# Causal mask of an attention block as one bf16 product per PSUM bank, and its score products 64 rows deep on the two halves of the TensorE rows

## The chip, the cores and the metric

One NeuronCore of one Trainium2 chip runs the whole program. The metric is the device time of one execution in microseconds (us). Names used below: PE is the matmul side of TensorE and PEld its weight loads, DVE is VectorE, ACT is ScalarE, POOL is GpSimd, SP is the engine that queues most DMAs. Each engine works through its own instructions in order; semaphores tie the engines together.

## The reference

A small language model layer: a token lookup, a bidirectional state-space block (32 sequences of 512 tokens), and then a transformer layer. Its attention is the part that the change touches. For every position of the 512, attention runs over the 32 sequences, with 4 key/value groups of 4 query heads each, head size 16:

```
qkv = ln1 @ qkv_weight.T            # ln1: layer norm of h
scores = einsum('bgqsd,bgtd->bgqst', q, k) * 16**-0.5
scores = where(tril, scores, finfo.min)
attn = softmax(scores)
ao = einsum('bgqst,bgtd->bgqsd', attn, v)
h1 = h + ao @ proj_weight.T
# then layer norm, router, top 2 of 8 experts, and the experts
```

## The kernel before, in words

Three stages follow one another: the state-space stage, the attention stage (`attention_stage`), and the expert stage, with a small routing stage ahead of the experts. The attention stage takes the 512 positions in 32 turns of BB = 16 positions. In a turn the functions named `slot` on each engine set the order by hand; the engines overlap work of neighbouring turns.

TensorE in a turn `slot(c)`: `scores(c)` (L1395), `turn_v(c)` (transposes of the values, L1385), `qk(c+1)` (projections of the next turn, L1376), `turn2(c-1)` (transposes of the normalised rows of the turn before, L1445), `ranks(c-2)` (L1466, L1468), `router(c-1)` (L1454), `turn_p(c)` (transposes of the probabilities, L1405), `products(c)` (L1424), `project(c)` (L1433), `turn1(c+2)` (L1366).

One score product treats one position: the stationary operand is `qt`, (64 + 32) rows by 128 columns (4 query heads of a group times 32 sequences), the moving operand is `kb`, (64 + 32) rows by 128 (4 groups times 32 sequences). The first 64 rows are the 4 groups of 16 head values, with the groups that don't belong set to zero in `kb`; the last 32 rows hold an identity in `qt` and the causal mask in `kb`, so that the product adds the mask. POOL writes these 32 rows once, ahead of the turns. Four positions share one PSUM bank `A[i]`; the four banks are done in the order BANKS = (2, 3, 0, 1), and each raises `s_ps` at its end. In the profile a f32 product is two instructions, so a turn has 32 of them.

VectorE: `add_projection(c-1)` (L1570), `stats2(c-1)` (L1576, L1580), `less_max` of the first two banks (L1542, L1545), `v_copy` (L1533), `normalise2(c-1)` (L1590), `less_max` of the other two banks, `sums` (L1552, L1555), `keep_logits(c-1)` (L1597), `next_rows` and `place` for the routing, `stats1(c+2)` (L1510), `first_input`, `pick_experts`, `normalise(c+2)` (L1525).

ScalarE: `exp` of the first two banks (L1279), four `q_copy(c+1)` (L1259, PSUM to `qt`, 64x512 each), `exp` of the other two banks, `x2t_copy(c-1)` (L1303), four copies of `k_copy(c+1)` with a scale column (L1267, PSUM to `kb`), `pt_copy(c)` (L1286), `vs_copy(c+1)` (L1274), `ao_copy(c)` (L1297, eight of 64x256), `lt_copy(c+2)` (L1251).

GpSimd: `scales2(c-1)` (L1192, L1194), `base(c-1)` (L1209), `normalise(c)` (L1203), `scales1(c+2)` (L1183 to L1187), and `send(c-2)`, eight indirect DMAs (L1216).

The waits around the change: `scores(c)` waits for all nine copies of its turn on the semaphore `qk_ok` (QK = 9) and raises `s_ps` four times; `products(c)` also counts `qk_ok`, since it overwrites the banks that `q_copy` reads; `less_max` waits for `s_ps`.

Of the kernel before, what the change touches and what calls it, by code (L numbers as in the profile page):

```python
# [19 lines left out]
BF16 = mybir.dt.bfloat16  # L20
I32 = mybir.dt.int32
U32 = mybir.dt.uint32
ALU = mybir.AluOpType
ACT = mybir.ActivationFunctionType
AX_X = mybir.AxisListType.X

P = 128
# [932 lines left out]
BB = 16  # L960
NG = 4
NQ = 4
HD = 16
S_A = 32
NE = 8
QK = NQ + NG + 1
QT = 3
BANKS = (2, 3, 0, 1)
AV_BANK = (0, 1, 3, 2)
V_BANK = (2, 3)  # L970
GD = NG * HD
# [10 lines left out]
MASKED = -2.0 ** 127  # L982


def attention_stage(nc, w, h1_dram, out, xd_dram, both_all):
# [8 lines left out]
    with ctx:  # L994
        def sb(name, shape, dt=F32):
            return ctx.enter_context(nc.sbuf_tensor(name, shape, dt))
# [4 lines left out]
        lnw = sb("a_lnw", [P, 2, KD])  # L1001
        lnb = sb("a_lnb", [P, 2, KD])
        ident = sb("a_ident", [P, P])
        cmask = sb("a_cmask", [P, S_A])
        vmask = sb("a_vmask", [P, NG * HD])
        gmask = sb("a_gmask", [GD, NG])
        nh = sb("a_nh", [P, TT])
# [7 lines left out]
        r1 = sb("a_r1", [P, NCH * TT])  # L1015
        core = sb("a_core", [P, TT, DM])
        lt = sb("a_lt", [P, KD, SEQ])
        qt = sb("a_qt", [GD + S_A, BB, NQ, S_A])
        kb = sb("a_kb", [GD + S_A, BB, NG, S_A])
        vs = sb("a_vs", [P, BB, NG, S_A])  # L1020
        vb = sb("a_vb", [P, BB, NG * HD])
        ss = sb("a_ss", [P, BB, NG, S_A])
# [36 lines left out]
        A = [ctx.enter_context(nc.psum_tensor(f"a_pa{i}", [P, SEQ], F32)) for i in range(4)]  # L1059
        B = [ctx.enter_context(nc.psum_tensor(f"a_pb{i}", [P, SEQ], F32)) for i in range(4)]  # L1060
# [4 lines left out]
        S = {n: ctx.enter_context(nc.semaphore("a_" + n)) for n in names}  # L1065
# [11 lines left out]
        def after(eng, name, value):  # L1077

            if not (isinstance(value, int) and value <= 0):
                eng.wait_ge(S[name], value)  # L1080
# [44 lines left out]
        def _(pool):  # L1125
# [4 lines left out]
            for tile, value in ((ident, 0.0), (cmask, 0.0), (vmask, 0.0), (gmask, 1.0)):  # L1130
# [11 lines left out]
                               pattern=[[-1, P]], channel_multiplier=1).then_inc(S["c0"], 1)  # L1142
            pool.wait_ge(S["c0"], done + 1)
            done += 1
            rows = slice(GD, GD + S_A)
            pool.affine_select(out=cmask[rows, :], in_=cmask[rows, :], compare_op=ALU.is_ge, fill=MASKED, base=0,
                               pattern=[[-1, S_A]], channel_multiplier=1).then_inc(S["c0"], 1)
            pool.wait_ge(S["c0"], done + 1)

            for n, (tile, of) in enumerate(((kb, cmask[rows, :]), (qt, ident[rows, rows]))):  # L1150
                pool.tensor_copy(tile[rows].rearrange("p b g t -> p (b g) t"),
                                 of.unsqueeze(1).to_broadcast([S_A, BB * NG, S_A])).then_inc(S["c0"], 1)
                pool.wait_ge(S["c0"], done + 2 + n)
            done += 3
            for q in range(NQ):
# [89 lines left out]
        def _(act):  # L1245
# [8 lines left out]
            def q_copy(c, q):  # L1254

                act.wait_ge(S["qk_ps"], QT * c + q // 2 + 1)
                after(act, "s_ps", 4 * c)
                rows = slice(GD * (q % 2), GD * (q % 2 + 1))
                act.activation(qt[0:GD, :, q, :], B[q // 2][rows, :].rearrange("p (b s) -> p b s", b=BB), ACT.Copy  # L1259
                               ).then_inc(S["qk_ok"], 1)  # L1260

            def k_copy(c):

                act.wait_ge(S["qk_ps"], QT * (c + 1))
                after(act, "s_ps", 4 * c)
                for g in range(NG):
                    act.activation(kb[0:GD, :, g, :], B[2][0:GD, :].rearrange("p (b s) -> p b s", b=BB), ACT.Copy,  # L1267
                                   scale=gmask[:, g:g + 1]).then_inc(S["qk_ok"], 1)

            def vs_copy(c):  # L1270
                act.wait_ge(S["qk_ps"], QT * (c + 1))
# [41 lines left out]
            for q in range(NQ):  # L1313
                q_copy(0, q)
# [36 lines left out]
        def _(pe):  # L1351
            mm = nc.tensor.matmul
# [35 lines left out]
            def scores(c):  # L1388
                pe.wait_ge(S["qk_ok"], QK * (c + 1))
                after(pe, "pt_ok", 4 * c)  # L1390
                for n, i in enumerate(BANKS):
                    if n == 2:
                        after(pe, "hh_ok", 2 * c)
                    for b in range(4):
                        o = mm(A[i][:, b * P:(b + 1) * P], qt[:, 4 * i + b].rearrange("p q s -> p (q s)"),  # L1395
                               kb[:, 4 * i + b].rearrange("p g t -> p (g t)"), start=True, stop=True)
                    o.then_inc(S["s_ps"], 1)

            def turn_p(c):
                for n, i in enumerate(BANKS):  # L1400
# [8 lines left out]
            def products(c):  # L1409
                for n, i in enumerate(BANKS):  # L1410
                    if n == 0:
                        pe.wait_ge(S["v_ok"], 2 * (c + 1))
                    if n < 2:
                        if c + 1 < NCH:
                            pe.wait_ge(S["qk_ok"], QK * (c + 1) + 2 * n + 2)
                    elif n == 2:
                        after(pe, "lg_ok", c)
                        if not (isinstance(c, int) and c < 2):
                            pe.wait_ge(S["rt"], ROUTES * (c - 2) + PICKS + 2)
                    elif c + 1 < NCH:  # L1420
                        pe.wait_ge(S["qk_ok"], QK * (c + 2))
                    pe.wait_ge(S["pt_ok"], 4 * c + n + 1)
                    for b in range(4):
                        o = mm(B[AV_BANK[n]][0:GD, b * P:(b + 1) * P], vb[:, 4 * i + b, :], pt[:, 4 * i + b, :],  # L1424
                               start=True, stop=True)
                    o.then_inc(S["av_ps"], 1)
# [830 lines left out]
```

## Time and profile before

| | |
|---|---|
| median of 3 runs | 4419.59 us (4418.56 to 4421.79) |
| span of the profiled execution | 4422.3 us |
| attention turns, first scores to the last turn's scores (31 turns) | 876.65 us |
| busy in that stretch | PE 798.88, PEld 667.62, DVE 732.92, ACT 538.04, POOL 520.10 us |
| granted TensorE clock in that stretch | 0.90 of full (full is 2.4 GHz, the other level is 1.2 GHz) |

"Busy" of PE counts pipelined matmuls from start to modelled end, so it is near the whole stretch whatever they do; idle gaps and the spacing of starts say more. A row of a timeline gives the start, the length of a run of equal instructions, the engine, the line, the operation, the tiles written and read, the shapes and the count. A row by stretch gives start and end, the length, the busy time (and count) of PE, PEld, DVE, ACT and POOL, the granted clock, the DMA share and GB/s. Brackets at the end of a timeline row give the idle time of the engine before it, and what ended that.

### The profile page before, as it was taken

To read this page: it belongs to the slowest core of one execution; us is meant where nothing else is said; L and a number is where in the kernel's file an instruction comes from. 1 tells how busy PE (TensorE), PEld (TensorE's weight loads), DVE (VectorE), ACT (ScalarE), POOL (GpSimd) and SP (SyncE) were. 2 spreads that over 40 slices of the span, in tenths; PEclk is the share of its full clock that TensorE was granted. 3 is DMA by queue.
4 is the path that set the end of the run, shared out by engine and by line. 5 is a ranking of instruction groups with operands and counts; after the bars stand their busy time and mean duration, and the time that the engine had idled before them with its cause. 6 is when DMAs were issued, how large, how long until landed. Compare 5 with 4: busy or idle time off the path is not lost. (4 is left out here: it accounts for less than half of the span.)

```text
span 4422.3 us, 69821 instructions
## 1 busy us (share of the span) xinstructions
PE 3980.4 (90%) x19212; PEld 2978.1 (67%) x19213; DVE 3702.1 (84%) x7005; ACT 2858.3 (65%) x4732; POOL 2328.0 (53%) x1953
## 2 busy tenths in 40 slices
PE   6999999999999999999999699998999379999998
PEld 4666666666666666666666477777777368888887
DVE  7999999999999999999999568888888446666666
ACT  5777777777777777777777566666665134454444
POOL 2445545454545445454545436665666435555555
PEclk8989889988989898899889789988998689999999
DMA  2222222112222222222122212222221155555555
GB/s 67 47 42 46 46 42 51 41 43 42 49 42 51 42 47 46 42 51 42 44 42 47 53 43 75 76 77 73 76 75 68 47 136 96 95 104 96 87 95 85
DMA packets 197949, 272.58 MB, mean 62 GB/s; under 512 B 23377, under 2 KB 142546, under 8 KB 197842
## 3 DMA queue, kind: packets, MB, share of 16 engines
q0 software_dynamic: 94720, 131.65, 17.1%
q1 hardware_dynamic: 99680, 137.43, 11.4%
q10 hardware_dynamic: 3442, 2.21, 0.2%
q8 instruction: 50, 0.82, 0.1%
q14 instruction: 57, 0.47, 0.0%
HBM read 121.07 MB, written 150.14 MB: 61 GB/s over the span
## 5 line engine op out<-in xcount | busy, mean ns | idle before, releaser
L608 PE MATMUL pj<-xt,win 128*128 128x512 f32 x3144 | 920.5, 452 | 12.2 <-DVE uc L793 10.1
L608 PEld LDWEIGHTS pj<-xt,win 128*128 128x128 f32 x3144 | 675.5, 217 | 199.3 <-issue 45.7
L1991 POOL DMA_INDIRECT out<-e_y,e_to x272 | 465.1, 1710 | 365.2 <-ACT e_y L2097 305.5
L300 POOL TENSOR_TENSOR r<-r,neg_half 128x4 f32<-128x4 f32 x64 | 90.8, 1419 | 844.5 <-ACT r L383 844.5
L793 DVE SCALAR_TENSOR_TENSOR uc<-pj,convw,uc 128x511 f32<-128x511 f32 (+2 forms) x780 | 516.8, 728 | 5.7 <-ACT uc L407 5.7
L656 PE MATMUL po<-yz,wout 128*128 128x512 f32 x1024 | 483.6, 628 | 28.3 <-ACT fb L486 28.3
L325 POOL TENSOR_TENSOR wk<-v,uc 128x512 f32<-128x512 f32 x260 | 332.9, 1280 | 246.5 <-DVE v L841 245.7
L2042 PE MATMUL e_p<-e_w,e_a 128*128 128x256 f32 x3264 | 410.4, 283 | 1.2 <-DVE e_a L2152 1.0
L656 PEld LDWEIGHTS po<-yz,wout 128*128 128x128 f32 x1024 | 198.6, 199 | 310.5 <-issue 308.6
L2030 PE MATMUL e_p<-e_xt,e_w 128*128 128x512 f32 x1632 | 391.3, 396 | 5.3 <-DVE e_xt L2144 2.7
L2042 PEld LDWEIGHTS e_p<-e_w,e_a 128*128 128x128 f32 x3264 | 387.6, 188 | 11.9 <-DVE e_a L2152 7.5
L2030 PEld LDWEIGHTS e_p<-e_xt,e_w 128*128 128x128 f32 x1632 | 304.4, 190 | 71.2 <-issue 7.0
L329 POOL TENSOR_TENSOR tp<-wk,bb 128x512 f32<-128x512 f32 x260 | 332.9, 1280 | 30.5 <-POOL wk L325 19.9
L2150 DVE CAST e_a<-e_af 128x512 fp32r<-128x512 f32 x272 | 117.3, 431 | 242.6 <-ACT e_af L2090 237.9
L677 PE MATMUL po<-wfus,fo 128*128 128x256 f32 x1024 | 238.1, 386 | 75.2 <-ACT fo L477 75.2
L1216 POOL DMA_INDIRECT expert_in<-a_xs,a_idx x256 | 249.5, 975 | 98.2 <-issue 79.2
L848 DVE TENSOR_TENSOR_SCAN tp<-y,tp 128x512 f32<-128x512 f32 x256 | 291.6, 1196 | 0.0
L677 PEld LDWEIGHTS po<-wfus,fo 128*128 128x128 f32 x1024 | 189.3, 190 | 151.4 <-ACT fo L477 128.2
L833 DVE SCALAR_TENSOR_TENSOR wk<-wk,lg 128x1024 f32<-128x1024 f32 x130 | 224.8, 1729 | 71.2 <-ACT lg L463 71.1
L2090 ACT ACTIVATE e_af<-e_p 128x512 f32<-128x512 f32 x272 | 162.1, 598 | 185.7 <-PE e_p L2030 184.2
L2097 ACT ACTIVATE e_y<-e_p,e_share 128x256 f32<-128x256 f32 x272 | 114.4, 472 | 235.8 <-PE e_p L2042 235.8
L415 ACT ACTIVATE zs<-pj 128x512 f32<-128x512 f32 x260 | 155.7, 599 | 169.2 <-PE pj L608 169.2
(247 smaller groups left out, 9155.6 us busy)
## 6 DMA issues: line engine op xcount, KB each, us to landing
e_x<-expert_in SPq DMA_DIRECT2D x138, 260.0 KB, 2.7
bb<-bc SPq DMA_DIRECT2D x65, 512.0 KB, 5.4
h_rows<-fb POOLq DMA_DIRECT2D x64, 512.0 KB, 6.3
h_rows<-h0c SPq DMA_DIRECT2D x32, 512.0 KB, 2.9
a_h<-h_rows SPq DMA_DIRECT2D x128, 128.0 KB
out<-a_bs SPq DMA_DIRECT2D x128, 128.0 KB
bc<-xd SPq DMA_DIRECT2D x65, 128.0 KB, 2.2
e_w1s<-in_moe_w POOLq DMA_DIRECT2D x10, 512.0 KB, 5.8
```

The lines of the kernel that those rows point to most:

```text
L325: pool.tensor_tensor(wk[:, m, :], v[:, m, :], uc[d][:, m, :], ALU.mult).then_inc(S["dtu_ok"], 1)
L329: pool.tensor_tensor(tp[:, m, :], wk[:, m, :], bb[d][:, 0, :], ALU.mult).then_inc(S["tp_ok"], 1)
L608: i = mm(pj[m][:], win[d][wp][:, k, c:c + P], xt[xp][:, k, :], start=(k == 0 and n == 0), stop=(k == KD - 1 and n == 2))
L656: i = mm(po[k][:], wout[d][:, m, k * P:(k + 1) * P], yz[:, m, :], start=(m == 0), stop=(m == MD - 1))
L677: i = mm(po[h][:, jj * DM:(jj + 1) * DM], fo[:, k, j * P:(j + 1) * P], wfus[d][:, k, :], start=(k == 0), stop=(k == KD - 1))
L793: stt(uc[d][:, m, to], pj[m][:, of], convw[d][:, m, tap:tap + 1], uc[d][:, m, to], ALU.mult, ALU.add).then_inc(S["cv"], 1)
L833: stt(wk[:, mm, :], wk[:, mm, :], 1.0, lg[:, mm, :], ALU.subtract, ALU.subtract).then_inc(S["g_ok"], 1)
L848: nc.vector.tensor_tensor_scan(tp[:, m, step], y[:, m, step], tp[:, m, step], 0.0, ALU.mult, ALU.add).then_inc(S["h_ok"], 1)
L1216: pool.indirect_dma_start(out=xd_dram, out_offset=bass.IndirectOffsetOnAxis(ap=idx[:, k, j:j + 1].bitcast(U32), axis=0), in_=xs[p][:, j, : ...
L1991: pool.indirect_dma_start(out=out, out_offset=bass.IndirectOffsetOnAxis(ap=to[n][:, j:j + 1].bitcast(U32), axis=0), in_=y[n][:, j, :], in_ ...
L2030: o = mm(p1[m][:], w1[i][wp][:, k, m * P:(m + 1) * P], xt[xp][:, k, :], start=(k == 0 and s == 0), stop=(k == KD - 1 and s == 2))
L2042: o = mm(p2[n][:, j, :], a[ap][:, m, (n * HT + j) * P:(n * HT + j + 1) * P], w2[i][wp][:, m, :], start=(m == 0 and s == 0), stop=(m == MF ...
```

## The change

The mask no longer rides in the depth of each product. Each bank first gets one bf16 product 32 rows deep and 512 columns wide: the identity repeated four times (`crow`) times the mask repeated sixteen times (`ccol`), with `start=True`. The 16 position products then add to it, 64 rows deep. `qt` and `kb` lose their 32 rows and hold half of the positions in rows 0 to 63 and the other half in rows 64 to 127; banks 2 and 3 are filled together, one product of the one half and one of the other in turn, then banks 0 and 1. Each copy to `qt` and `kb` is split in two of half the size, so ScalarE has 16 where it had 8, and QK is 17 in place of 9. POOL fills two smaller bf16 tables in place of the 32 rows of `kb` and `qt`.

```diff
-QK = NQ + NG + 1
+QK = 2 * NQ + 2 * NG + 1
-        cmask = sb("a_cmask", [P, S_A])
+        cmask = sb("a_cmask", [S_A, S_A], BF16)
+        crow = sb("a_crow", [S_A, NQ, S_A], BF16)
+        ccol = sb("a_ccol", [S_A, 4 * NG, S_A], BF16)
-        qt = sb("a_qt", [GD + S_A, BB, NQ, S_A])
-        kb = sb("a_kb", [GD + S_A, BB, NG, S_A])
+        qt = sb("a_qt", [2 * GD, BB // 2, NQ, S_A])
+        kb = sb("a_kb", [2 * GD, BB // 2, NG, S_A])
...
-            for n, (tile, of) in enumerate(((kb, cmask[rows, :]), (qt, ident[rows, rows]))):
-                pool.tensor_copy(tile[rows].rearrange("p b g t -> p (b g) t"),
-                                 of.unsqueeze(1).to_broadcast([S_A, BB * NG, S_A])).then_inc(S["c0"], 1)
+            for n, (tile, of, times) in enumerate(((ccol, cmask[:], 4 * NG), (crow, ident[0:S_A, 0:S_A], NQ))):
+                pool.tensor_copy(tile[:], of.unsqueeze(1).to_broadcast([S_A, times, S_A])).then_inc(S["c0"], 1)
...
-                act.activation(qt[0:GD, :, q, :], B[q // 2][rows, :].rearrange("p (b s) -> p b s", b=BB), ACT.Copy
-                               ).then_inc(S["qk_ok"], 1)
+                each = B[q // 2][rows, :].rearrange("p (i h b s) -> p h i b s", i=2, h=2, s=S_A)
+                for h in range(2):
+                    dst = qt[GD * h:GD * (h + 1), :, q, :].rearrange("p (i b) s -> p i b s", i=2)
+                    act.activation(dst, each[:, h], ACT.Copy).then_inc(S["qk_ok"], 1)
...
+                each = B[2][0:GD, :].rearrange("p (i h b s) -> p h i b s", i=2, h=2, s=S_A)
                 for g in range(NG):
-                    act.activation(kb[0:GD, :, g, :], B[2][0:GD, :].rearrange("p (b s) -> p b s", b=BB), ACT.Copy,
-                                   scale=gmask[:, g:g + 1]).then_inc(S["qk_ok"], 1)
+                    for h in range(2):
+                        dst = kb[GD * h:GD * (h + 1), :, g, :].rearrange("p (i b) s -> p i b s", i=2)
+                        act.activation(dst, each[:, h], ACT.Copy, scale=gmask[:, g:g + 1]).then_inc(S["qk_ok"], 1)
...
-                for n, i in enumerate(BANKS):
-                    if n == 2:
+                for pair in (1, 0):
+                    if pair == 0:
                         after(pe, "hh_ok", 2 * c)
+                    for h in range(2):
+                        mm(A[2 * pair + h][:], crow[:].rearrange("p q s -> p (q s)"),
+                           ccol[:].rearrange("p b t -> p (b t)"), start=True, stop=False)
                     for b in range(4):
-                        o = mm(A[i][:, b * P:(b + 1) * P], qt[:, 4 * i + b].rearrange("p q s -> p (q s)"),
-                               kb[:, 4 * i + b].rearrange("p g t -> p (g t)"), start=True, stop=True)
-                    o.then_inc(S["s_ps"], 1)
+                        for h in range(2):
+                            rows = slice(GD * h, GD * (h + 1))
+                            o = mm(A[2 * pair + h][:, b * P:(b + 1) * P],
+                                   qt[rows, 4 * pair + b].rearrange("p q s -> p (q s)"),
+                                   kb[rows, 4 * pair + b].rearrange("p g t -> p (g t)"), start=False, stop=(b == 3))
+                            if b == 3:
+                                o.then_inc(S["s_ps"], 1)
...
-                            pe.wait_ge(S["qk_ok"], QK * (c + 1) + 2 * n + 2)
+                            pe.wait_ge(S["qk_ok"], QK * (c + 1) + 4 * n + 4)
```

## Rows read from the trace of the kernel before

**Rows 1.** The page's first line, the span of the profiled execution.
```profile
span 4422.3 us, 69821 instructions
```
**Rows 2.** Busy time by stretch: the 31 attention turns, then three single turns.
```profile
2557.53:3434.18 876.65, 798.88 (x5212) 667.62 (x5211) 732.92 (x2379) 538.04 (x927) 520.10 (x533) 0.90 0.21 70
...
2977.98:3003.76 25.78, 23.58 (x172) 19.05 (x171) 24.05 (x80) 17.12 (x31) 15.76 (x17) 1.00 0.22 74
...
2920.87:2948.52 27.65, 24.88 (x172) 20.78 (x171) 24.27 (x81) 17.34 (x31) 17.30 (x18) 0.94 0.22 78
...
2948.52:2977.98 29.46, 26.44 (x173) 22.26 (x172) 24.43 (x81) 17.45 (x31) 18.49 (x19) 0.88 0.22 77
```
**Rows 3.** Waits of 2600 to 3400 us: who for whom, total, times, longest.
```profile
PE a_pb L1454 <- ACT a_x2t L1303: 70.2, 28, 3.4
...
DVE a_xs L1590 <- DMA expert_in<-a_xs,a_idx: 14.6, 17, 2.3
```
**Rows 4.** Timeline of one turn, TensorE: scores, turn_v, qk, then router.
```profile
2920.87 3.74 PE L1395 MATMUL a_pa<-a_kb,a_qt 96*128 96x128 f32 x32
...
2924.54 1.20 PE L1385 MATMUL a_pb<-a_ident,a_vs 64*128 64x64 f32 x16
...
2925.67 5.42 PE L1376 MATMUL a_pb<-a_lt,a_wq 128*128 128x512 f32 x12
...
2935.06 1.65 PE L1454 MATMUL a_pb<-a_wr,a_x2t 128*128 128x8 f32 x13 [2.77 <-ACT a_x2t L1303]
```
**Rows 5.** The same turn on VectorE, from project to x2t.
```profile
2920.80 1.40 DVE L1576 BATCH_NORM_STATS2 a_st<-a_hh 128x6 f32<-128x256 f32 x4
...
2922.60 0.66 DVE L1542 TENSOR_REDUCE a_mx<-a_pa 128x16 f32<-128x512 f32 x1
...
2925.28 1.29 DVE L1533 TENSOR_TENSOR a_vb<-a_pb,a_vmask 128x512 f32<-128x512 f32 x2
2927.07 3.15 DVE L1590 TENSOR_SCALAR a_xs<-a_hh,a_mv,a_rr 128x256 f32<-128x256 f32 x4 [0.50 <-DMA expert_in<-a_xs,a_idx]
```
**Rows 6.** The same turn on GpSimd: the start of scales2.
```profile
2925.45 0.19 POOL L1192 TENSOR_SCALAR a_ve<-a_mv 128x4 f32<-128x4 f32 x1
```
**Rows 7.** ScalarE: copies of k, pt and ao, then q, exp and x2t.
```profile
2905.68 2.39 ACT L1267 ACTIVATE a_kb<-a_pb,a_gmask 64x512 f32<-64x512 f32 x4
...
2910.41 0.60 ACT L1286 ACTIVATE a_pt<-a_pa 128x512 f32<-128x512 f32 x1 [2.33 <-PE a_pa L1405]
...
2915.39 3.19 ACT L1297 ACTIVATE a_ao<-a_pb 64x256 f32<-64x256 f32 x8
...
2929.40 1.21 ACT L1259 ACTIVATE a_qt<-a_pb 64x512 f32<-64x512 f32 x2 [0.51 <-PE a_pb L1376]
2931.58 0.63 ACT L1279 ACTIVATE a_ss<-a_ss 128x512 f32<-128x512 f32 x1 [0.97 <-DVE a_ss L1545]
...
2933.56 1.45 ACT L1303 ACTIVATE a_x2t<-a_pa,a_lnb,a_lnw 128x512 f32<-128x512 f32 x2
```
**Rows 8.** Busy time by stretch: PE's gap ahead of the router, and `turn_p`.
```profile
2932.60:2935.06 2.46, 0.00 (x1) 0.01 (x1) 2.39 (x6) 2.13 (x4) 1.23 (x2) 1.00 0.25 90
...
2937.04:2940.46 3.42, 3.42 (x19) 3.25 (x19) 2.90 (x20) 1.87 (x4) 0.85 (x1) 0.58 0.29 101
```
**Rows 9.** Timeline of the state-space stage: products 128 rows deep, then 16.
```profile
1524.24 0.84 PE L608 MATMUL pj<-xt,win 128*128 128x512 f32 x3
1525.01 1.99 PE L625 MATMUL pj<-xd,wdt 16*128 16x512 f32 x8
```
**Rows 10.** Two lines' matmuls: shortest, median and longest record in ns.
```profile
L625 PE MATMUL pj<-xd,wdt x520: 587/587/692, 46.0 to 2477.8; 16*128 16x512 f32 x174
...
L1395 PE MATMUL a_pa<-a_kb,a_qt x1024: 273/275/421, 2557.5 to 3437.6; 96*128 96x128 f32 x171
```
**Rows 11.** Timeline ahead of the first turn.
```profile
2551.35 2.40 ACT L1267 ACTIVATE a_kb<-a_pb,a_gmask 64x512 f32<-64x512 f32 x4 [0.51 <-PE a_pb L1376]
...
2559.48 0.69 DVE L1542 TENSOR_REDUCE a_mx<-a_pa 128x16 f32<-128x512 f32 x1 [12.35 <-PE a_pa L1395]
```

More of the change, by code:

```diff
@@ L1144, in _ @@
             done += 1
-            rows = slice(GD, GD + S_A)
-            pool.affine_select(out=cmask[rows, :], in_=cmask[rows, :], compare_op=ALU.is_ge, fill=MASKED, base=0,
+            pool.affine_select(out=cmask[:], in_=cmask[:], compare_op=ALU.is_ge, fill=MASKED, base=0,
                                pattern=[[-1, S_A]], channel_multiplier=1).then_inc(S["c0"], 1)
             pool.wait_ge(S["c0"], done + 1)
-            for n, (tile, of) in enumerate(((kb, cmask[rows, :]), (qt, ident[rows, rows]))):
-                pool.tensor_copy(tile[rows].rearrange("p b g t -> p (b g) t"),
-                                 of.unsqueeze(1).to_broadcast([S_A, BB * NG, S_A])).then_inc(S["c0"], 1)
+            for n, (tile, of, times) in enumerate(((ccol, cmask[:], 4 * NG), (crow, ident[0:S_A, 0:S_A], NQ))):
+                pool.tensor_copy(tile[:], of.unsqueeze(1).to_broadcast([S_A, times, S_A])).then_inc(S["c0"], 1)
                 pool.wait_ge(S["c0"], done + 2 + n)
```

## The prediction

> **What bounds the kernel now.** I read the stretch of the attention turns first, since nothing outside it is touched. Its 31 turns take 876.65 us, 28.3 us each, with PE busy for 91% of it and VectorE for 84% [rows 2]. Near-full PE is not proof that PE sets the turn, so the list of waits comes next: PE has one large wait, 70.2 us in 28 turns, and it is ahead of the router, for the last copy `x2t` of ScalarE [rows 3]. The reader is to see in the timeline what lies between the scores and that wait. Scores start at 2920.87, `turn_v` at 2924.54, `qk` at 2925.67, and with `turn2` and `ranks` PE is through at about 2932.3; then it stands for 2.77 us and starts the router at 2935.06 [rows 4]. Whatever is saved in the scores lengthens this gap unless VectorE waits for the scores.
>
> VectorE does not. It starts `less_max` at 2922.60, right behind the statistics and with no idle time, although the first bank was done at 2920.87 + 7 x 0.112 + 0.275 = 2921.93 (0.112 us from start to start is (3.74 - 0.275) / 31) [rows 4, 5, 10]. So the first bank has a slack of 0.67 us. The four steps of `less_max` and `v_copy` run to 2926.57 back to back, then comes `normalise2`, which in 17 of 28 turns waited for the scatter or for POOL behind it, 14.6 us, 0.86 us a time [rows 3, 5]. In the turn shown POOL, which issues eight scatters ahead of it, comes to `scales2` only at 2925.45, and `normalise2` rests on it [rows 6]. After it VectorE's second `less_max`, `exp` and `x2t_copy` follow without a break to the router [rows 5, 7]. So two loops hold a turn: from `project` through VectorE and ScalarE to the router and back through PE, and from the router through VectorE and POOL's scatters to `scales2`. Neither holds the scores, but for 0.67 us of slack in the first.
>
> The third thing is TensorE's clock. It is granted at 0.90 over the stretch, which is half speed (1.2 GHz in place of 2.4) for a fifth of it; a turn with the clock full throughout took 25.78 us, one at 0.94 took 27.65, one at 0.88 took 29.46 [rows 2]. In the turn shown PE stands still at the full clock ahead of the router, and in `turn_p`, after the router, the mean is 0.58 [rows 8]: the clock falls behind the gap, where PE is on the path.
>
> **The change part by part.** *The score products.* Every bank now holds 4 products of two instructions, as before, but rows 0 to 63 and 64 to 127 go in turn, to two banks. The trace has such a case: `dt_proj` gives four products 16 rows deep at rows 64 and 96 in turn. Its eight instructions of 512 columns took 1.99 us [rows 9]. One after the other they would take 0.587 + 7 x 0.44 = 3.7 us, with 0.44 = (5.42 - 0.59) / 11 from `qk` [rows 4, 10]. So two row groups do run side by side, with f32 and with their weight loads. Hence 16 steps of 0.112 = 1.79 us in place of 32 x 0.112 = 3.58. Bounds: 1.79 and 3.58; I take the lower, as L625 is nearest in kind.
>
> *The mask.* Four bf16 products, 512 columns, 32 deep. No row has one. Lower bound 0.11 us (the pace of 128 columns), upper 0.44 (f32 in two passes per instruction, L1376). The nearest row is L608, one pass over 512 columns: three in 0.84 us with a record of 0.39 for the last, 0.225 from start to start [rows 9]. I take 0.22 each, 0.88 in all (0.44 to 1.76).
>
> *Changes of row depth.* After the third L608 (1524.24 + 3 x 0.225 = 1524.91) the 16-row products start at 1525.01, 0.10 later, and the first record is 0.105 longer (692 against 587 ns), its weight load no longer hidden [rows 9, 10]. Between scores and `turn_v` it is 2924.54 - (2920.87 + 3.58) = 0.09 us [rows 4]. So 0.2 us ahead of each f32 group and some 0.15 ahead of a bf16 one. New are four such (128 to 32, 32 to 64, twice); the one ahead of `turn_v` goes, since both are 64 deep. Sum for the block: 4 products of mask 0.88 + 1.79 + 2 x 0.35 = 3.37 us until `turn_v`, against 3.67: PE gains 0.3 us a turn, where a count of instructions would have said 0.9.
>
> The Trainium skill's page "TensorE: Matmul & The Clock Gate", section "Measured speedup vs the span model", has four row groups of 512 columns gain 3.07 of 4. By that the steps would cost 1.3 times 0.112, an estimate from that page, the block 3.9 us and the result about 3 us more; the row of L625 shows no such loss, and I go by the row.
>
> *When the first bank is done.* It now shares its time with the second: 0.15 + 0.44 + 0.2 + 8 x 0.112 + 0.16 (the rest of the last record) = 1.85 us after the block's start, against 1.06. VectorE asks for it at 1.73 [rows 4, 5]. That is 0.12 us too late, and with the 0.03 us from a record's end to the reader 0.15. The second bank is there at once, and `v_copy`, which now starts 0.04 us after the eighth transpose of `turn_v`, gets its bank earlier, so of the 0.15 about 0.10 is left. It counts in the 11 of 28 turns in which `normalise2` doesn't wait [rows 3]: 31 x 11/28 x 0.10 = 1.2 us. If the masks cost 0.11 it is nothing; if they cost 0.44 it is 0.5 us a turn in those, 6 us.
>
> *ScalarE's copies.* A copy of 64x512 has a pace of 0.60 (2.39 / 4), one of 64x256 of 0.40 (3.19 / 8) [rows 7]. `q_copy` takes 4 x 0.40 per projection in place of 1.21: the last pair ends 0.4 us later, but `qk` is 0.3 earlier, and `exp` behind it had 0.97 us idle. `k_copy` takes 3.2 in place of 2.4 us; the next, `pt_copy`, waited 2.33 us for PE. With the clock full the router and the first bank of `turn_p` take half as long and that cover shrinks to a few tenths; the first `pt_copy` may then slip by 0.5, which costs at most 0.5 us in a turn of the 25.78 kind [rows 2]. Taken as nothing, at most 3 us over all. `vs_copy` and what waits for it move with `pt_copy` only.
>
> *The start.* Ahead of the first turn nothing covers this: scores wait for all 17 copies, and `k_copy` is on the path (2551.35, 2.40 us) [rows 11]: +0.8 us. The first `less_max` then waits on the first bank, which came 1.95 us after the scores' start at 2557.53, TensorE being slower there than later [rows 2, 11]; in proportion (1.85 / 1.06) it is 1.5 us later, of which the second bank, already there, gives some back: +1.4. POOL's smaller tables end up to 3 us earlier, but VectorE's first step waited for the load of h, so no gain.
>
> *The clock.* PE's gap grows by 0.3 us where loop two holds. If all of it lengthened the half-speed time, that would be 0.15 us a turn, 4.6 us; if nothing, 0. I take 2 us.
>
> **Sum.** 4422.3 [rows 1] + 1.2 + 0.8 + 1.4 + 2 = 4427.7 for a profiled execution. The median of the runs is 2.7 us below the profiled span, so 4425.0.
>
> **The rivals.**
> *A: the two halves don't overlap* when each is 64 rows deep. A pair of banks then takes 0.15 + 0.44 + 0.2 + 16 x 0.112 = 2.58 us, the block 5.2; `turn_v` and `v_copy` come 1.5 us late. 11 of 28 turns pay 1.45, the others 0.6 after their slack: 0.93 a turn, 29 us, less what a shorter gap gives back in clock, up to 11. About 4442. L625 speaks against it. Chance 0.08.
> *B, slower: the clock.* The half-speed stretches shift against the turns. From 27.65 to 29.46 us a turn costs 1.8 us; with 8 turns more of the second kind it is 14 us: 4439. It decides from two more such turns, since 3.4 us are left to the bound. For it: a longer gap can only bring the fall nearer to the router. The Trainium skill's page "TensorE: Matmul & The Clock Gate", section "HAM oscillation — how this bites in real kernels", says that idle gaps between bursts send the clock to half; by that the gap is paid in every turn, and the trace agrees in so far as two of the three single turns shown have a part at half speed [rows 2]. Chance 0.20.
> *C, faster: the clock or PE pays back.* Eight turns fewer of the slow kind, or the 0.3 us of each turn reaching the end (31 x 0.3 = 9.3): 4425 - 14 = 4411, or 4422.3 - 2.7 - 9.3 = 4410. For it: PE is busy for 91%. Against: its wait of 70.2 us. Chance 0.20.
> The forecast itself, nothing reaches the end but the small terms: 0.52.
>
> **How the numbers follow.** Within 0.2% of before (8.8 us, 4410.8 to 4428.4, about what a measurement can tell) lies the forecast: 0.52. Slower are A and B, 0.28; faster is C, 0.20. The range takes in most of B and C and the masks' upper bound, 4409 to 4441.
>
> **What would show it.** Right: L1395's successor in pairs of starts a few ns apart, 16 steps of 0.11 us; masks of 0.22 us; `turn_v` 3.4 us after the block's start; `less_max` idle some 0.1 us for the first bank; the wait ahead of the router at 2.8 us or more a turn in place of 2.5; `exp` and `pt_copy` still waiting for others. Wrong: `turn_v` later than 3.67, a turn's mean off 28.3 us by more than 0.3, or a mean clock other than 0.89 to 0.91.

## The result, and the profile after

The changed kernel takes 4438.65 us (median of 4 runs, 4436.05 to 4442.37), against 4419.89 us for the kernel before run beside it: a ratio of 1.0042, 95% interval 1.0028 to 1.0056. It is slower by 18.8 us, 0.42%. I had said 4425, within 4409 to 4441, and "no change" as the likeliest.

The profiled execution of after took 4436.8 us, 14.5 more than that of before [rows 1]. First the busy time by stretch (start:end, length, busy time and count of PE, PEld, DVE, ACT, POOL, granted clock, DMA share, GB/s): all 31 turns, the first turn, the 30 others, two single turns, and last the two pieces of the first turn at half speed, the one around the first scores and one behind them.

```profile
span 4436.8 us, 70333 instructions
...
2561.16:3450.85 889.69, 801.30 (x5335) 635.79 (x5335) 730.75 (x2379) 599.63 (x1175) 519.13 (x532) 0.88 0.20 69
...
2561.16:2592.66 31.50, 28.34 (x137) 20.38 (x137) 15.91 (x39) 18.50 (x37) 6.23 (x7) 0.70 0.00 1
2592.66:3450.85 858.19, 772.96 (x5199) 615.41 (x5199) 714.83 (x2341) 581.13 (x1139) 512.90 (x525) 0.88 0.21 72
...
2905.81:2933.36 27.55, 24.40 (x175) 19.31 (x175) 24.33 (x80) 19.03 (x38) 17.19 (x19) 0.94 0.22 75
2933.36:2962.83 29.47, 26.11 (x175) 20.70 (x175) 24.47 (x80) 19.73 (x39) 18.43 (x19) 0.88 0.23 78
...
2556.20:2573.30 17.10, 14.02 (x66) 9.12 (x67) 7.65 (x13) 7.62 (x11) 0.09 (x1) 0.50 0.00 1
...
2580.11:2586.93 6.82, 5.81 (x26) 5.44 (x27) 3.18 (x14) 6.62 (x12) 2.15 (x4) 0.50 0.00 0
```

The same split of before, which [rows 2] gave only as one sum, and the two pieces around its first scores:

```profile
2557.53:2581.74 24.21, 22.73 (x133) 17.57 (x133) 15.81 (x39) 16.28 (x29) 6.22 (x7) 0.93 0.00 1
2581.74:3434.18 852.44, 776.15 (x5081) 650.05 (x5079) 717.11 (x2342) 521.76 (x899) 513.88 (x526) 0.90 0.21 72
...
2554.20:2561.00 6.80, 5.20 (x25) 5.23 (x26) 1.38 (x2) 4.36 (x5) 0.00 (x0) 0.50 0.00 0
2561.00:2581.70 20.70, 19.22 (x117) 14.05 (x117) 14.39 (x37) 13.95 (x26) 6.22 (x7) 1.00 0.00 1
```

The reader is to see three things. The first turn alone went from 24.21 to 31.50 us, 7.3 us, half of the 14.5. It ran at half speed twice: through the scores, `turn_v` and most of `qk` (the last row above), and once more behind a stop of 1.88 us in `turn_p`, where before had no second fall. 3.0 of the 7.3 us lie ahead of `turn_p`, 4.3 behind its start. The 30 others cost 5.75 us more, 0.19 us each, at a clock of 0.88 in place of 0.90. And single turns of one clock cost what they did: 27.55 at 0.94 and 29.47 at 0.88, against 27.65 and 29.46 [rows 2]; there are more of the slower kind (of the 30 later turns seven at 0.93 or more in place of eleven). The rest of the 14.5 us: the attention's first transposes already start 1.93 us later, ahead of anything that was changed; from there to the first scores it is 17.57 us in place of 15.87, 1.70 more; behind the last scores 2.2 us less. The medians differ by 4 us more than the two profiled executions, which is within what a kernel's runs differ by among themselves (6.3 us for after).

The timeline of a steady turn of after (start, length, engine, line, what it writes and reads, count, and in brackets the idle time before it), TensorE, then VectorE, then ScalarE (its rows belong to the same stretch, 14 us later):

```profile
2905.81 0.60 PE L1399 MATMUL a_pa<-a_ccol,a_crow 32*128 32x512 bf16 x2
2906.34 1.16 PE L1404 MATMUL a_pa<-a_kb,a_qt 64*128 64x128 f32 x16
2907.44 0.60 PE L1399 MATMUL a_pa<-a_ccol,a_crow 32*128 32x512 bf16 x2
2907.97 1.16 PE L1404 MATMUL a_pa<-a_kb,a_qt 64*128 64x128 f32 x16
2908.97 1.15 PE L1389 MATMUL a_pb<-a_ident,a_vs 64*128 64x64 f32 x16
...
2919.82 2.14 PE L1465 MATMUL a_pb<-a_wr,a_x2t 128*128 128x8 f32 x16 [3.15 <-ACT a_x2t L1307]
...
2905.05 0.69 DVE L1581 TENSOR_TENSOR a_hh<-a_pa,a_fi 128x512 f32<-128x512 f32 x1 [1.04 <-PE a_pa L1444]
...
2907.53 0.69 DVE L1553 TENSOR_REDUCE a_mx<-a_pa 128x16 f32<-128x512 f32 x1
...
2919.66 3.92 ACT L1272 ACTIVATE a_kb<-a_pb,a_gmask 64x256 f32<-64x256 f32 x8
2923.61 0.60 ACT L1290 ACTIVATE a_pt<-a_pa 128x512 f32<-128x512 f32 x1
```

The change does what it says. Sixteen instructions take 1.16 us, where they took 15 x 0.112 + 0.275 = 1.96: the two halves of the rows do work side by side. The block lasts 2908.97 - 2905.81 = 3.16 us until `turn_v`, 0.5 less than before [rows 4]. And the waits of 2600 to 3400 us (engine, tile and line, for whom, total us, times, longest) show where it goes:

```profile
PE a_pb L1465 <- ACT a_x2t L1307: 76.2, 28, 3.4
...
DVE a_xs L1601 <- DMA expert_in<-a_xs,a_idx: 13.8, 16, 4.3
```

TensorE waits 76.2 us ahead of the router in place of 70.2, and the wait of the VectorE loop is about what it was (14.6) [rows 3]. Of the 0.5 us saved in a turn, 0.2 (6.0 us in 28 waits) lies in the longer gap, and the 30 turns became no shorter; what the gap does to the clock is the subject of the experiments.

### The profile page after: what moved, and what is told of

Same layout as the page of the kernel before. It is cut to its first block and busy times, and to the rows that moved or that the text cites. A ratio compares the mean times of both kernels' runs of the same rounds, so it can differ in the third digit from the quotient of the medians.

```text
span 4436.8 us, 70333 instructions
## 1 busy us (share of the span) xinstructions
PE 3981.3 (90%) x19340; PEld 2943.6 (66%) x19341; DVE 3702.1 (83%) x7005; ACT 2921.9 (66%) x4988; POOL 2324.1 (52%) x1953
```

## The experiments

My theory after the result: the copies cost little, the loss is TensorE's clock, in the first turn and in the longer gap of each later one. Rivals: the split copies on ScalarE; the mask products as work; a first bank that comes too late for VectorE. The kernel before, run beside e1 to e4, e5 to e8 and e9 to e12, took 4419.66, 4422.53 and 4423.68 us, so ratios are what to compare. Two edits recur: *first*, six products that nothing uses, behind `qk(0)`, where TensorE had stood idle ahead of the first scores; *gap*, one to five such products in the idle time ahead of the router. Both are pure extra work.

**Split copies alone (e1), on before.** Each copy of `q_copy` and `k_copy` in two of 64x256, all into rows 0 to 63, the score products as before:

```diff
-QK = NQ + NG + 1
+QK = 2 * NQ + 2 * NG + 1
+                each = B[q // 2][rows, :].rearrange("p (i h b s) -> p h i b s", i=2, h=2, s=S_A)
+                for h in range(2):
+                    dst = qt[0:GD, :, q, :].rearrange("p (i h b) s -> p h i b s", i=2, h=2)[:, h]
+                    act.activation(dst, each[:, h], ACT.Copy).then_inc(S["qk_ok"], 1)
```

> The kernel before, with each copy to qt and kb split in two of 64x256 and nothing else changed: scores stay 96 rows deep with the f32 mask. Theory 1 (most of the loss is spent once, ahead of and in the first turn, the copies being 1.7 us of it, and a turn later on hides them): 1.5 to 4 us over before, 4421 to 4424, the 30 later turns within 0.05 us of before. Theory 2 (ScalarE's copies hold the later turns, where pt_copy now starts right behind k_copy): 0.2 us in each of 30 turns, 6 us more, 4428 or over.

Measured: 4422.4 us, ratio 1.0000 (0.9991 to 1.0009), though the two medians lie 2.7 us apart. Its turns and its first `k_copy`:

```profile
2559.43:2584.66 25.23, 23.09 (x134) 17.89 (x133) 15.81 (x39) 17.10 (x37) 6.23 (x7) 0.92 0.00 1
2584.66:3437.61 852.95, 774.53 (x5080) 649.24 (x5079) 712.98 (x2342) 545.22 (x1139) 514.32 (x526) 0.90 0.21 72
...
2552.66 2.99 ACT L1272 ACTIVATE a_kb<-a_pb,a_gmask 64x256 f32<-64x256 f32 x8 [0.40 <-PE a_pb L1380]
```

30 turns cost 852.95 us against 852.44: with 23 us more on ScalarE (545.22 against 521.76) the turns don't move. The copies as the cause of the 18.8 us are out; at most 0.9 thousandths, 4 us, fit the interval.

**The mask products left out (e2), on after.** The kernel computes unmasked attention.

```diff
-                    for h in range(2):
-                        mm(A[2 * pair + h][:], crow[...], ccol[...], start=True, stop=False)
...
-                                   kb[rows, 4 * pair + b]..., start=False, stop=(b == 3))
+                                   kb[rows, 4 * pair + b]..., start=True, stop=True)
```

> The changed kernel without the mask products (the mask is left out, so attention isn't causal); the score products in pairs stay. The block should fall from 3.16 us to about 2.0 and the first bank come 0.8 us before VectorE asks. If VectorE's late first bank and the block's length set the loss: 30 turns x 0.1 to 0.2 plus some 3 us in the first turn less than the changed kernel, 4430 to 4433. If TensorE's clock sets it, the gap ahead of the router grows by 1.1 us and the turns get slower by up to 0.5 us each: 4440 to 4453, with a mean clock below that of the changed kernel in the turns.

Measured: 4441.9 us, ratio 1.0050 (1.0036 to 1.0064). Less work, and not faster than after.

```profile
2559.75:2584.30 24.55, 20.92 (x133) 15.66 (x132) 15.71 (x39) 18.48 (x37) 6.19 (x7) 0.93 0.00 1
2584.30:3454.87 870.57, 754.62 (x5079) 620.74 (x5079) 714.24 (x2341) 578.73 (x1139) 512.66 (x525) 0.85 0.20 71
...
PE a_pb L1462 <- ACT a_x2t L1307: 88.7, 27, 3.4
```

The first turn is back at 24.55 us and a clock of 0.93. The 30 others take 870.57, 12.4 us more than after, with 88.7 us of waiting ahead of the router (76.2) and a clock of 0.85 (0.88). So the mask products are what the first turn pays for, and in the later turns nothing is gained by taking them out: the gap gets wider, and the turns longer. TensorE stands still for 6.00 us ahead of the first turn both here and in after, so the longer wait there is not what holds the first turn's clock down. The other runs agree: where nothing fills TensorE's time ahead of the scores, the first turn's clock is 0.69 to 0.71 in the four runs with mask products (after, e4, e6, e8), and 0.91 to 0.93 in the five without (before, e1, e2, e5, e11).

**Work for TensorE ahead of the first scores (e3), on after.**

```diff
             qk(0)
+            for _ in range(6):
+                mm(A[0][:], wq[:, 0, 0, :], lt[:, 0, :], start=True, stop=True)
```

> The changed kernel with six more f32 products of 128 rows and 512 columns (their result is not used) while TensorE waits for the first turn's copies. Theory 1 (the first turn took 31.5 us in place of 24.2 because the clock stood at 1.2 GHz through scores, turn_v and most of qk): the first turn takes 24 to 27 us, 5 to 7 us less than the changed kernel, 4431 to 4434. Theory 2 (the first turn is long for the mask's and the late bank's sake): 0 to 1 us less, 4437 to 4439.

Measured: 4430.25 us, ratio 1.0023 (1.0014 to 1.0032), against 1.0042 for after.

```profile
2557.42:2581.68 24.26, 20.63 (x137) 14.41 (x137) 15.71 (x39) 18.79 (x37) 6.21 (x7) 1.00 0.01 2
2581.68:3447.62 865.94, 786.77 (x5200) 629.67 (x5199) 710.46 (x2341) 581.42 (x1139) 513.34 (x526) 0.86 0.21 71
...
PE a_pb L1465 <- ACT a_x2t L1307: 71.0, 27, 3.4
```

The first turn now has the full clock throughout and takes 24.26 us in place of 31.50. In this one execution the later turns, whose code is that of after, took 865.94 us against 858.19; so the sum over 30 turns moves by some 8 us between two executions of like code, and the first turn's share is read from the medians (8.4 us) and from e6 and e10 below. By the same token the 5.75 us of after's later turns could be chance if they stood alone; that the later turns did lose is shown by the median here, 1.0023 with the first turn mended. The wait ahead of the router is 71.0 us, hardly more than before (70.2), and yet the clock is 0.86 in place of 0.90: the length of the gap is not all that sets the clock in the later turns, and what else does isn't shown.

**The same on before (e7).** The edit of e3 on the kernel before.

> The kernel before with six more products (not used) while TensorE waits for the first turn's copies. If the start matters only as time at half speed, the first turn, 24.2 us with 3.5 us of its own at half speed, loses about 1.7 us: 4416 to 4419, hardly to be told from before. The gain of 8 us that the same products gave the changed kernel isn't to be had here. If they gain 5 us or more here too, the changed kernel's long first turn was not the change's doing.

Measured: 4423.45 us, ratio 1.0001 (0.9992 to 1.0011).

```profile
2558.85:2581.38 22.53, 21.05 (x134) 15.89 (x133) 15.71 (x39) 16.54 (x29) 6.22 (x7) 1.00 0.00 1
2581.38:3433.99 852.61, 776.80 (x5081) 651.68 (x5080) 715.25 (x2342) 521.11 (x899) 512.58 (x525) 0.90 0.21 72
```

Before had only 1.7 us to gain in its first turn (24.21 to 22.53). The fault that e3 mends is one of the change.

**One half after the other (e4), on after.** The two loops of the score products change places, so a bank gets its four products one behind the other, the first bank is ready early, and the halves of the rows overlap much less.

```diff
-                    for b in range(4):
-                        for h in range(2):
+                    for h in range(2):
+                        for b in range(4):
```

> The changed kernel with the two halves of the rows one after the other (all of bank 2, then all of bank 3), so that products of the same rows follow each other. If the overlap of the two halves is real and worth 0.11 us a step, the block grows from 3.16 to about 4.9 us, turn_v and v_copy come late by over 1 us, the gap ahead of the router shrinks by as much, and the time is 8 to 20 us over the changed kernel, 4447 to 4459. The first bank itself would come early, 1.3 us after the start. If the pairs gain nothing, the block and the time stay those of the changed kernel.

Measured: 4431.77 us, ratio 1.0029 (1.0018 to 1.0039).

```profile
2560.06:2593.12 33.06, 29.92 (x137) 22.23 (x136) 15.90 (x39) 18.48 (x37) 6.23 (x7) 0.69 0.00 1
2593.12:3450.40 857.28, 782.38 (x5200) 625.96 (x5199) 712.96 (x2341) 577.84 (x1139) 514.02 (x526) 0.92 0.21 72
...
2904.88 1.71 PE L1404 MATMUL a_pa<-a_kb,a_qt 64*128 64x128 f32 x16
...
2707.02:2733.70 26.68, 24.05 (x175) 18.74 (x174) 23.32 (x80) 18.99 (x39) 16.64 (x18) 1.00 0.22 75
```

Sixteen instructions take 1.71 us in place of 1.16, and the program is no slower: 857.28 against 858.19 us for the 30 turns, and the intervals of the two ratios overlap. I had expected 4447 to 4459. The overlap of the halves is real, and nothing of it reaches the end. A turn with the full clock throughout takes 26.68 us here (the last row), where it took 25.78 before [rows 2], so 1.1 us more TensorE time isn't free; a higher clock over the 30 turns (0.92 against 0.88) makes up for it.

**The gap ahead of the router filled: before (e5) and after (e6).** Three products of 384 columns that nothing uses, in `slot`, ahead of `router(c - 1)`:

```diff
+            def fill(c):
+                pe.wait_ge(S["v_ok"], 2 * values_before(c, 1))
+                for _ in range(3):
+                    mm(B[3][:, P:], wq[:, 0, 0, :], lt[:, 0, P:], start=True, stop=True)
...
+                    fill(c - 1)
                     router(c - 1)
```

> The kernel before with three f32 products of 128 rows and 384 columns (results not used) in TensorE's gap ahead of the router, 1.9 us of more work a turn. If the fall of the clock behind that gap is what sets a turn (25.8 us at the full clock, 27.5 with 3.4 us at half, 28.7 with 6.8), the half-speed time goes from 5.8 us a turn to under 3, and the time falls by 20 to 45 us, to 4375 to 4400. If TensorE's work sets the turn, or the clock only mirrors the length of a turn, 1.9 us more a turn gives the same or up to 57 us more, 4420 to 4477.

> The changed kernel with the same three products in the gap. If the clock is what the shorter scores cost, the two kernels meet once the gap is filled: as fast as the kernel before with its gap filled, to within 10 us (the first turn's 7 to 11 us at the half clock stay). If the change costs by another way (the late first bank, ScalarE's 16 copies), it stays as much behind as it is now, 19 us, or falls back further, since faster turns leave ScalarE's k_copy less cover.

Measured: on before 4406.5 us, ratio 0.9962 (0.9949 to 0.9976), the lowest of this study; on after 4415.59 us, 0.9984 (0.9975 to 0.9993). Of e5:

```profile
2558.47:2583.14 24.67, 23.20 (x134) 18.04 (x133) 15.81 (x39) 16.27 (x29) 6.22 (x7) 0.91 0.00 1
2583.14:3417.26 834.12, 795.08 (x5260) 633.37 (x5259) 722.72 (x2342) 517.10 (x899) 510.69 (x523) 0.96 0.22 74
```

and of e6:

```profile
2560.32:2592.61 32.29, 28.73 (x137) 20.60 (x137) 15.91 (x39) 18.49 (x37) 6.23 (x7) 0.69 0.00 1
2592.61:3430.48 837.87, 785.85 (x5379) 589.60 (x5379) 725.12 (x2341) 574.44 (x1139) 513.68 (x525) 0.95 0.21 74
...
2936.11 2.18 PE L1472 MATMUL a_pb<-a_lt,a_wq 128*128 128x384 f32 x6
```

More work for TensorE, and 18 to 20 us less in the 30 turns of either kernel, at a clock of 0.96 and 0.95. I had expected more of e5, 4375 to 4400. The clock is thus the price of the gap. With it filled, after costs 3.75 us more than before in the later turns where it cost 5.75, and the first turn (32.29) stays as bad as it was.

**One of them, with the first turn mended (e9), on after.** *First*, and `range(1)` in *gap*.

> The changed kernel with the six unused products ahead of the first turn and one unused f32 product of 128 rows and 384 columns, 0.64 us, in each gap, so that TensorE's gap and its work from scores to router are as long as in the kernel before (0.51 us of scores less, 0.64 more). If what is left of the loss in the later turns is the longer gap's clock, the half-speed time per turn comes back from 6.8 to 7.9 us to some 5.8 and the time to 4420 to 4425: before, plus 2 to 3 us for the 16 copies at the start, and plus 2 for the late first bank. If it is the late bank or the copies in the later turns, it stays at the 4430 of the run with the first turn mended.

Measured: 4420.28 us, ratio 0.9992 (0.9983 to 1.0001).

```profile
2558.93:2583.21 24.28, 20.63 (x137) 14.41 (x137) 15.72 (x39) 18.82 (x37) 6.22 (x7) 1.00 0.01 2
2583.21:3433.58 850.37, 778.28 (x5259) 601.38 (x5259) 717.39 (x2341) 578.68 (x1139) 514.50 (x526) 0.91 0.21 73
...
PE a_pb L1465 <- ACT a_x2t L1307: 62.0, 28, 2.6
```

This is the test of the steady turns by dose. A product takes 0.645 us (six instructions last 2.18 us in e6, ten 3.47 in e11, so two are half of the difference), 19 us more work in 30 turns, and against e3, which differs by it alone, the ratio falls from 1.0023 to 0.9992, about 14 us. TensorE's wait fell from 71.0 to 62.0 us and the clock rose from 0.86 to 0.91. Work put into the gap is thus worth more than it costs. With the gap no longer than before's, the 30 turns take 850.37 us against 852.44, with the mask products, the 16 copies and the later first bank all in place. That a gap longer by the change's 0.2 us costs in turn is inferred from this; the same product on before was not tried.

**Three of them, with the first turn mended (e10), on after.** *First* and `range(3)`.

> The changed kernel with both: six products ahead of the first turn and three in each gap. If the 9 us that lie between the two kernels with filled gaps are the first turn's clock (7 us) and the copies (2 us), it comes to 4407 to 4411, equal to the kernel before with its gap filled to within 0.1%. If the change costs something else in each turn, it stays at 4415.

Measured: 4410.51 us, ratio 0.9970 (0.9958 to 0.9982).

```profile
2559.79:2584.06 24.27, 20.62 (x137) 14.40 (x137) 15.73 (x39) 18.81 (x37) 6.21 (x7) 1.00 0.01 2
2584.06:3422.92 838.86, 791.46 (x5379) 597.03 (x5379) 721.85 (x2341) 575.51 (x1139) 513.00 (x524) 0.95 0.21 73
```

e6 and e10 differ by *first* alone, and here the later turns agree (837.87 and 838.86): 8.0 us less in the first turn, 0.0014 less in the ratio, 6 us.

**Five of them: before (e11), and after with the first turn mended (e12).**

> The kernel before with five unused products in each gap, 3.2 us, longer than the mean gap of 2.9 us. Three took the half-speed time from 5.8 to 2.4 us a turn and 16 us off. If the clock can be held altogether, the half-speed time goes to under 1 us a turn, and what is left is the loop through VectorE, ScalarE, GpSimd and the router: 4395 to 4405. If the two more products reach into the router's time more than they save in clock, 4410 to 4425.

> The changed kernel with six products ahead of the first turn and five in each gap, whose mean is 3.2 us here. If shorter scores are worth something once the clock doesn't fall, this is the place: the same as the kernel before with five, or up to 5 us faster, 4390 to 4405. If scores are off the path whatever the clock does, and the copies and the late bank cost 2 us each, it is 2 to 6 us behind that one.

Measured: 4411.46 us, 0.9972 (0.9963 to 0.9983), and 4410.6 us, 0.9971 (0.9959 to 0.9982). The 30 later turns of e11, its five products in one turn and its wait of VectorE, then the turns of e12 and two waits of TensorE:

```profile
2586.55:3424.24 837.69, 811.67 (x5380) 622.22 (x5379) 722.53 (x2342) 512.97 (x899) 512.68 (x524) 1.00 0.22 73
...
2930.81 3.47 PE L1461 MATMUL a_pb<-a_lt,a_wq 128*128 128x384 f32 x10
...
DVE a_xs L1596 <- DMA expert_in<-a_xs,a_idx: 51.7, 27, 5.0
```

```profile
2586.10:3424.81 838.71, 794.21 (x5499) 579.44 (x5499) 725.12 (x2341) 573.17 (x1139) 514.09 (x525) 1.00 0.21 74
...
PE a_pb L1435 <- ACT a_pt L1290: 20.0, 26, 0.8
PE a_pb L1435 <- ACT a_vs L1278: 12.2, 26, 0.5
```

Both lie above the 4405 that I had set as the upper end for a full clock. With the clock at 1.00 in both, the change of the scores is worth nothing either way: 838.71 against 837.69 us, ratios equal to 0.0001. But from 2600 to 3400 us TensorE waits 32.2 us here for ScalarE ahead of `products`, for `pt_copy` and `vs_copy`, which now come late behind `k_copy`'s eight; in e11 it never does, and in after neither. So once the clock is held, the split copies may well eat the time that the shorter scores save, and e12 doesn't clear them; it shows only that the whole change costs nothing more than it saves there. For the turns as they were, e9 is the witness (3.9 us of such waits). Nor is a full clock itself the aim: e5 with three products and 0.96 is as fast (0.9962, the intervals overlap). What binds e11 then isn't shown: the wait of VectorE for the scatters grew from 14.6 us [rows 3] to 51.7, which speaks for the loop of VectorE and POOL.

**Mask product per bank, but the 64-deep products in one half of the rows (e8), on before.** Bank after bank, eight copies, tables as in after:

```diff
+                    mm(A[i][:], crow[:]..., ccol[:]..., start=True, stop=False)
                     for b in range(4):
                         o = mm(A[i][:, b * P:(b + 1) * P], qt[:, 4 * i + b]..., kb[:, 4 * i + b]...,
-                               start=True, stop=True)
+                               start=False, stop=(b == 3))
```

> The kernel before with the mask as one bf16 product per bank, the score products 64 rows deep in rows 0 to 63 only, bank after bank, eight copies as before. The block should be 4 x (0.15 + 0.22 + 0.2 + 8 x 0.112) = 5.9 us or, if products of one row group cost no change of depth, 5.3, in place of 3.7. The first bank is on time, the later ones and v_copy come late. If the gap's clock is what counts, 1.6 to 2.2 us more of work a turn cost little, under 10 us, since the gap shrinks; if VectorE's wait counts, 11 of 28 turns pay 1.5 us and the others 0.7: 30 us, 4450.

Measured: 4460.65 us, ratio 1.0080 (1.0067 to 1.0094). The 30 later turns, a stretch from a router to the next turn's scores, and two pieces within these scores:

```profile
2591.65:3473.03 881.38, 845.24 (x5200) 655.93 (x5199) 693.18 (x2341) 513.04 (x899) 513.26 (x524) 0.88 0.20 70
...
2924.85:2942.56 17.71, 17.71 (x106) 15.96 (x106) 13.59 (x62) 10.83 (x19) 12.16 (x14) 0.81 0.25 90
...
2940.15:2942.56 2.41, 2.41 (x18) 2.02 (x17) 2.27 (x9) 0.87 (x2) 1.80 (x3) 1.00 0.27 97
2942.96:2946.30 3.34, 3.34 (x14) 2.68 (x14) 1.19 (x2) 1.29 (x3) 3.19 (x4) 0.53 0.11 40
```

PE is busy for 100% of all three stretches, 17.71 us without a stop ahead of the fall, and the clock falls from 1.00 to 0.53 between the two pieces. That is more than I had expected (under 10 us, or 30): the mask as a product of its own without the pairing costs 35 us, 8 of them in the first turn (31.97 us). The 30 later turns take 881.38 us in place of 858.19 in after, so the pairing pays for most of what the mask products cost there, though the number of copies and the order of the banks differ too.

## Why the prediction was right and wrong

**The sum.** 18.8 us by the medians. By the runs, 8.4 of it is the first turn (after against e3; 6 by e6 against e10), and e3 still stands 10.2 us above before, 1.7 of it from the start. Those 10.2 shrink to 3.5 with three products in the gap (e10 against e5, intervals overlapping) and to nothing with five (e12 against e11), in spite of the waits for ScalarE there: the greater part is clock. The forecast of 4425 was some 14 us low. The range reached the time through rival B's 4439, and that B's number is met to 1 us is luck: nearly half of the 18.8 us is the first turn, which B didn't have.

**First turn, forecast +1.4 us, measured +7.3: the step that failed.** I scaled the delay of the first bank by how slow TensorE was there, and took for granted that the clock comes back as in before, 3.5 us into the scores (at 2561.00). In after it stayed at 0.50 from 2556.20 to 2573.30, through scores, `turn_v` and most of `qk`, and fell again from 2580.11 to 2586.93. e2 puts this on the four mask products: the 64-deep pairs without them gave 0.93 and 24.55 us. Whether it is their 32 rows, their type or the pauses at each change of depth isn't settled.

**The clock in the later turns, forecast +2 us, measured some 8** (10.2 less the start's 1.7; 5.75 in the one profiled execution). The place was right (behind the gap ahead of the router), the size was not. I bounded it by "half of the growth of the gap", 4.6 us. The trace had no ground for that bound: the time that a stretch at half speed costs isn't tied to how much longer the gap became, and e9 shows one product of 0.645 us in each gap moving the kernel by 14 us. The test I set, a mean clock of 0.89 to 0.91, came out as 0.88. The mean of all 31 turns moved by 0.42 us (28.28 to 28.70), outside the 0.3, but more than half of that is the first turn. For the later turns rival B, to which I had given 0.20, names the mechanism: more turns of the slow kind. The Trainium skill's page "TensorE: Matmul & The Clock Gate", section "HAM oscillation — how this bites in real kernels", has gaps between bursts send the clock to half. By e5, e6 and e9 the runs agree (clock 0.96, 0.95 and 0.91 with the gap filled in part); e8 shows a fall without a gap.

**The start, forecast +0.8 us, measured +1.7.** The term of the pace of copies was mis-sized. I took 0.40 us from `ao_copy` for a copy of 64x256; `k_copy` with its scale column took 3.92 / 8 = 0.49, so 1.5 us more than before [rows 11]. In e1, where all copies stay in rows 0 to 63, it is 2.99 / 8 = 0.37. In the turns the split copies are covered (e1), at the start they are not.

**The block, forecast 3.37 us, measured 3.16.** The two products of a pair start 6 to 7 ns apart; two banks are 8 steps in 1.16 us, (1.16 - 0.27) / 7 = 0.127 us each with about 0.1 more ahead of the second step in the sum, so (1.16 - 0.27 - 0.1) / 7 = 0.113 without it: my 0.112. The Trainium skill's page "TensorE: Matmul & The Clock Gate", section "Measured speedup vs the span model", has four row groups gain 3.07 of 4, by which a step would have taken 1.3 times 0.112, an estimate from that page; the trace shows no such loss. Masks start 0.23 us apart (my 0.22). A change of depth cost some 0.17 us for an f32 group, 0.08 to its start and 0.1 ahead of its second step, where I had 0.2, and 0.1 for a mask, where I had 0.15; and I had counted two changes to a mask, of which the first lies ahead of the block's start. So the block was too dear by 0.2.

**The first bank, forecast 0.10 us late, measured 0.08.** `less_max` starts 2907.53 - 2905.05 = 2.48 us after `add_projection`, the turn's first step on VectorE, against 2922.60 - 2920.20 = 2.40 in the turn of [rows 5], whose `add_projection` is

```profile
2920.20 0.69 DVE L1570 TENSOR_TENSOR a_hh<-a_pa,a_fi 128x512 f32<-128x512 f32 x1 [1.03 <-PE a_pa L1433]
```

Over 30 turns 0.08 us is 2.4 us at most. What of it reaches the end, my 1.2 us, can't be told from nothing: the 30 turns of e12 and e11 differ by 1.0 us.

**Hidden as said:** `q_copy`, `k_copy` and POOL's tables. `pt_copy` now starts right behind `k_copy` with no idle time (it had waited 2.33 us [rows 7]), so that cover is used up, but TensorE wasn't delayed by it. With the gap filled it is: 3.9, 11.2 and 32.2 us of waits in e9, e10 and e12, the slip of `pt_copy` that I had named for turns at the full clock and taken as nothing.

**Rival A** (halves don't overlap, 4442) is out by the pairs. e4 takes much of the overlap away (1.71 us in place of 1.16; one after the other would be 1.96) and is no slower than after. It doesn't make A true, since its first bank comes early, where A's comes late; but for the TensorE time alone A's price was too high. I had let the clock give back up to 11 us there; in e4 it gave back all that the longer block took.

## What to carry to other kernels

Where TensorE waits once a turn and its clock falls behind that wait, shortening its work is worth nothing and can cost: here a block 0.5 us shorter left the kernel 0.23% slower even with the first turn mended (e3), and three unused products in the gap made the kernel before 0.38% faster (e5). Price a change by what it does to the gap, and test it by putting spare work there before the real work is rewritten. At the start of a stage, look at whether TensorE's first products will bring the clock up; a few products of full depth ahead of them took 6 to 8 us off.

## What the runs showed of the hardware

- TensorE fully busy is not enough for the full clock. In after, 17.1 us around the first scores stayed at 1.2 GHz, PE busy for 14.02 of them (all but the 3.08 us ahead of 2559.28); in e8 the clock fell from 1.00 to 0.53 within products 64 rows deep, with PE busy throughout. I had expected a fall only behind idle time. In e2, whose first scores start at the same half speed but have no products 32 rows deep, the full clock came back within the scores (0.93 over the turn).
- Two groups of 64 rows with f32 operands, 128 columns and their own weight loads run side by side with no loss that the trace shows: a pair takes 0.112 us from start to start, as one instruction did before; 16 instructions take 1.16 us, against 1.71 with one half mostly after the other.
- Copies of 64x256 by ScalarE from PSUM with a scale column followed each other at 0.49 us where every second one writes other rows than it reads, and at 0.37 us in e1, where none does. The copies in e1 also lay their results out otherwise, so which of the two it is stays open.

**What stays open.** Whether the depth of the mask products, their type or the pauses around them hold the clock down; a product of the mask 128 rows deep would help to tell, and it wasn't tried. Why e3's later turns have a lower clock than before's with a gap hardly longer. Whether e4's order is in truth a few us faster than that of after: 1.0018 to 1.0039 and 1.0028 to 1.0056 overlap. And the start of the first scores itself moves by over 4 us between executions (2557.53 in before, 2562.04 in e11) through stages that nobody touched.
